# Score units in bursts of three instead of pairs, and four gates made by GpSimd

## The reference

```python
x = L0_attn_query
xn = _layernorm(x, axis=-1)
s = _L0_attn_ref(xn, ..., L0_attn_Wqkv, L0_attn_Wproj, L0_attn_bproj)   # softmax(q k / 4) v, then Wproj
g = _silu(_L0_ffn_ref(xn, ..., L0_ffn_proj1, L0_ffn_proj1_bias, L0_ffn_proj2, L0_ffn_proj2_bias, L0_ffn_gate_w))
x = x + s * g
```

## Time and profile before

| | us |
|---|---|
| median of 3 runs | 140.52 (140.23 to 141.25) |
| profiled execution | 139.67 |
| its span, first to last instruction | 137.9 |
| TensorE busy | 123.3 (89%) |
| VectorE busy | 88.0 (64%) |
| ScalarE busy | 75.9 (55%) |
| GpSimd busy | 50.8 (37%) |

### The profile page before, as it was taken

The page is one execution under the profiler, slowest core; times in us unless marked ns, Lnnn a source line. Parts: engine busy times, 40 slices in busy tenths (PEclk is TensorE's granted clock), DMA queues, the critical chain, the costliest instruction groups (busy, mean ns, idle before and its releaser), DMA issues.

```text
span 137.9 us, 2606 instructions
## 1 busy us (share of the span) xinstructions
PE 123.3 (89%) x980; PEld 93.9 (68%) x980; DVE 88.0 (64%) x178; ACT 75.9 (55%) x115; POOL 50.8 (37%) x53
## 2 busy tenths in 40 slices
PE   6669979999999699999999995899999999999640
PEld 5359868988899498886776783575666657656340
DVE  0658964300004599999996999096567838857563
ACT  3054359879971101137747432969779698779010
POOL 3268205999991000006466620299021000022300
PEclk9999999999999999999999999999999999999975
DMA  4899799999999950000000003500000100100202
GB/s 128 220 422 420 186 161 174 170 187 190 200 198 203 198 99 15 0 5 2 0 0 0 12 5 114 197 0 13 11 0 31 49 0 19 62 2 18 65 2 76
DMA packets 7553, 13.29 MB, mean 96 GB/s; under 512 B 1012, under 2 KB 2676, under 8 KB 7284
## 3 DMA queue, kind: packets, MB, share of 16 engines
q1 hardware_dynamic: 7108, 12.85, 38.9%
q10 hardware_dynamic: 432, 0.27, 1.1%
HBM read 5.51 MB, written 1.05 MB: 48 GB/s over the span
## 4 chain that ended last, share of the span: by engine, by line
PE 66%; DVE 15%; ACT 6%; issue 5%; DMA 5%; SPq 1%; ACTq 0%; DVEq 0%
PE bank L574 45%; PE bank L690 9%; DVE negm L491 8%; PE bank L662 6%; PE bank L642 6%; DMA wqkv_raw<-wqkv 5%; ACT PT L419 3%; DVE cd L508 2%; DVE yh L535 1%; ACT cTh L431 1%; DVE fin L553 1%; ACT xTh L363 1%; DVE rc L511 1%; SPq L247 1%; ACT wqh L353 0%
## 5 line engine op out<-in xcount | busy, mean ns | idle before, releaser
L491 DVE TENSOR_REDUCE negm<-bank 128x4 f32<-128x1024 f32 x32 | 37.1, 1218 | 20.1 <-PE bank L642 20.0
L419 ACT ACTIVATE PT<-bank 128x1024 f32<-128x1024 f32 x32 | 30.9, 1018 | 7.5 <-PE bank L662 7.5
L328 POOL TENSOR_TENSOR hTl<-hG,hTh 128x512 fp32r<-128x512 f32 x16 | 20.3, 1298 | 26.7 <-ACT hTh L405 26.7
L338 POOL TENSOR_TENSOR bg<-gate,bps 128x256 f32<-128x256 f32 x8 | 6.1, 762 | 38.6 <-DVE gate L459 29.9
L690 PE MATMUL bank<-PT,VA 128*17 128x256 f32 x256 | 16.9, 382 | 0.0
L574 PE MATMUL bank<-w2h,hTh 128*128 128x256 f32 x64 | 14.8, 313 | 1.8 <-DVE yh L535 1.6
L425 ACT ACTIVATE th<-yh 128x256 f32<-128x256 f32 x8 | 3.3, 417 | 22.9 <-DVE yh L535 22.9
L508 DVE STREAM_TRANSPOSE cd<-bank 128x256 f32<-128x256 f32 x16 | 7.2, 448 | 13.3 <-PE bank L690 13.3
L662 PE MATMUL bank<-qs,ks 50*128 50x256 f32 x128 | 12.9, 311 | 2.4 <-DVE negm L491 1.9
L574 PEld LDWEIGHTS bank<-w2h,hTh 128*128 128x128 f32 x64 | 9.7, 190 | 7.1 <-issue 6.1
L401 ACT ACTIVATE hG<-bank,b1s 128x512 f32<-128x512 f32 x16 | 11.0, 690 | 5.5 <-PE bank L574 5.5
(11 more groups left out here) (72 smaller groups left out, 205.2 us busy)
## 6 DMA issues: line engine op xcount, KB each, us to landing
qs<-stage SPq DMA_DIRECT2D x12, 256.0 KB, 10.6
ks<-stage SPq DMA_DIRECT2D x12, 256.0 KB, 16.1
w_raw<-w SPq DMA_DIRECT2D x2, 1024.0 KB, 10.3
xs<-x SPq DMA_DIRECT2D x4, 256.0 KB, 5.9
xb<-x SPq DMA_DIRECT2D x1, 1024.0 KB, 5.2
out<-fin SPq DMA_DIRECT2D x8, 128.0 KB, 1.7
wqkv_raw<-wqkv SPq DMA_DIRECT2D x3, 256.0 KB, 6.8
wps<-wp SPq DMA_DIRECT2D x8, 32.0 KB, 8.7
```

The costliest lines, as they stand in the source:

```text
L328: nc.gpsimd.tensor_tensor(hTl[:, n % FC, :], hG[:, n % FC, :], hTh[:, n % FC, :].bitcast(f32), ALU.subtract).then_inc(h_lo, 1)
L338: nc.gpsimd.tensor_tensor(bg[:, u % 2, :], gate[:, u, :], bps[:], ALU.mult).then_inc(bg_done, 1)
L419: nc.scalar.activation(PT[:, w % 4], scores_of(*s), ACT.Exp).then_inc(exp_done, 1)
L491: nc.vector.tensor_reduce(negm[:, j, :, :, s[1] % 2, b].rearrange("p q a -> p a q"), scores_of(*s), axis=AX.X, op=ALU.max, negate=True).th ...
```

## The change

1. `build_order` cuts the 32 score units into bursts of three (ten of three and one of two) and spreads the same filler over the 11 bursts. MT 0 and MT 1 are put ahead of the scores of a burst, two bursts behind the one that has their last maximum.
2. GpSimd makes the gates of tiles 0 to 3, as th + 1 and then times yh, in its own loop over the list, between the low parts of F1. VectorE keeps those of tiles 4 to 7. The semaphore gate_done becomes gate_first and gate_late, and the final product waits for the gate explicitly.

```diff
--- before.py
+++ after.py
@@ -20,6 +20,7 @@
 STM = STK + 2
 WARM = 5
 AHEAD = 6
+BURST = 3
 VW = HN + 1
 PAIRS = [(j, b) for half in range(2) for j in range(HP // 2) for b in (2 * half, 2 * half + 1)]
 
@@ -40,17 +41,17 @@
     filler = [(s, 1) for s in ffn[:4 * TT // 2]] + [(("F1", n), 1.9) for n in range(FC, 2 * FC)]
     filler += [(s, 1) for s in ffn[4 * TT // 2:4 * TT // 2 + AHEAD]]
     ffn = ffn[4 * TT // 2 + AHEAD:]
-    share = sum(w for _, w in filler) / len(PAIRS)
-    at = 0
-    for n in range(len(PAIRS)):
+    bursts = [range(n, min(n + BURST, 2 * len(PAIRS))) for n in range(0, 2 * len(PAIRS), BURST)]
+    share = sum(w for _, w in filler) / len(bursts)
+    at, turn = 0, [[], []]
+    for n, burst in enumerate(bursts):
         while filler and at < (n + 1) * share - 0.5:
             step, w = filler.pop(0)
             order.append(step)
             at += w
 
-        order += [("S", 2 * n), ("S", 2 * n + 1)]
-        if n >= 2 and PAIRS[n - 2][1] == B - 1 and PAIRS[n - 2][0] < 2:
-            order.append(("MT", PAIRS[n - 2][0]))
+        order += [("MT", j) for j in turn.pop(0) if j < 2] + [("S", u) for u in burst]
+        turn.append([PAIRS[u // 2][0] for u in burst if u % 2 and PAIRS[u // 2][1] == B - 1])
     assert not filler
     for g in range(GROUPS):
         j, b = divmod(g, B)
@@ -189,8 +190,9 @@
         m_rows = [sem(f"m_rows{j}") for j in range(HP // 2)]
         pv_made, cd_out, rc_done, norm_done = (sem(n) for n in ("pv_made", "cd_out", "rc_done", "norm_done"))
         turned, ct_hi, ct_lo, wp_hi, wp_lo = (sem(n) for n in ("turned", "ct_hi", "ct_lo", "wp_hi", "wp_lo"))
-        f2_made, b2_half, yh_done, th_done, gate_done, bg_done, xb_done = (
-            sem(n) for n in ("f2_made", "b2_half", "yh_done", "th_done", "gate_done", "bg_done", "xb_done"))
+        f2_made, b2_half, yh_done, th_done, gate_first, gate_late, bg_done, xb_done = (
+            sem(n) for n in ("f2_made", "b2_half", "yh_done", "th_done", "gate_first", "gate_late", "bg_done", "xb_done"))
+        th_plus = sem("th_plus")
         pj_made, gated, fin_done = sem("pj_made"), sem("gated"), sem("fin_done")
 
 
@@ -234,6 +236,10 @@
 
         def scores_of(*s):
             return bank[:, home[s][0]:home[s][0] + 2, :].rearrange("p a (q c) -> p a q c", q=2)
+
+        def gate_of(u):
+
+            return (gate_first, u + 1) if u < TT // 2 else (gate_late, u - TT // 2 + 1)
 
         block = ctx.enter_context(nc.Block())
 
@@ -323,16 +329,24 @@
                 fs = slice(4 * q, 4 * q + 4)
                 nc.gpsimd.tensor_tensor(w2l[:, fs, :], w2_raw[:, fs, :], w2h[:, fs, :].bitcast(f32),
                                         ALU.subtract).then_inc(w2_lo, 1)
-            for n in range(2 * FC):
-                pool.wait_ge(h_hi, n + 1)
-                nc.gpsimd.tensor_tensor(hTl[:, n % FC, :], hG[:, n % FC, :], hTh[:, n % FC, :].bitcast(f32),
-                                        ALU.subtract).then_inc(h_lo, 1)
+            for s in order:
+                if s[0] == "F1":
+                    n = s[1]
+                    pool.wait_ge(h_hi, n + 1)
+                    nc.gpsimd.tensor_tensor(hTl[:, n % FC, :], hG[:, n % FC, :], hTh[:, n % FC, :].bitcast(f32),
+                                            ALU.subtract).then_inc(h_lo, 1)
+                elif s[0] == "F2" and s[2] == 3 and s[1] < TT // 2:
+                    u = s[1]
+                    pool.wait_ge(th_done, u + 1)
+                    nc.gpsimd.tensor_scalar_add(th[:, u % 2, :], th[:, u % 2, :], 1.0).then_inc(th_plus, 1)
+                    pool.wait_ge(th_plus, u + 1)
+                    nc.gpsimd.tensor_tensor(gate[:, u, :], th[:, u % 2, :], yh[:, u % 2, :], ALU.mult).then_inc(gate_first, 1)
             pool.wait_ge(wp_hi, 1)
             nc.gpsimd.tensor_tensor(wpl[:], wps[:], wph[:].bitcast(f32), ALU.subtract).then_inc(wp_lo, 1)
             pool.wait_ge(x_again, 16)
             pool.wait_ge(bias_in, 48)
             for u in range(TT):
-                pool.wait_ge(gate_done, u + 1)
+                pool.wait_ge(*gate_of(u))
                 if u >= 2:
                     pool.wait_ge(xb_done, u - 1)
                 nc.gpsimd.tensor_tensor(bg[:, u % 2, :], gate[:, u, :], bps[:], ALU.mult).then_inc(bg_done, 1)
@@ -421,7 +435,7 @@
                     u = s[1]
                     act.wait_ge(yh_done, u + 1)
                     if u >= 2:
-                        act.wait_ge(gate_done, u - 1)
+                        act.wait_ge(*gate_of(u - 2))
                     nc.scalar.activation(th[:, u % 2, :], yh[:, u % 2, :], ACT.Tanh).then_inc(th_done, 1)
                 elif s[0] == "TURN":
                     kc, j = s[1:]
@@ -457,7 +471,7 @@
                 dve.wait_ge(yh_done, u + 1)
                 dve.wait_ge(th_done, u + 1)
                 nc.vector.scalar_tensor_tensor(gate[:, u, :], th[:, u % 2, :], 1.0, yh[:, u % 2, :],
-                                               ALU.add, ALU.mult).then_inc(gate_done, 1)
+                                               ALU.add, ALU.mult).then_inc(gate_late, 1)
 
             nc.vector.memset(warm[:], 0.0).then_inc(warm_set, 1)
             norm_stats(0)
@@ -531,10 +545,10 @@
                         dve.wait_ge(v_made, 4)
                     dve.wait_ge(f2_made, u + 1)
                     if u >= 2:
-                        dve.wait_ge(gate_done, u - 1)
+                        dve.wait_ge(*gate_of(u - 2))
                     nc.vector.scalar_tensor_tensor(yh[:, u % 2, :], bank_of("F2", u, 0)[:, 0:E], 0.5, b2s[:],
                                                    ALU.mult, ALU.add).then_inc(yh_done, 1)
-                    if u >= 1:
+                    if u > TT // 2:
                         finish_gate(u - 1)
                 elif s[0] == "GATE":
                     finish_gate(TT - 1)
@@ -546,6 +560,7 @@
                 elif s[0] == "PJ" and s[2] == KC - 1:
                     u = s[1]
                     dve.wait_ge(pj_made, u + 1)
+                    dve.wait_ge(*gate_of(u))
                     dve.wait_ge(xb_done, u + 1)
                     if u >= 4:
                         dve.wait_ge(stored[u - 4], 16)
```

## The result

The changed kernel takes 148.55 us (median of 4 runs, 147.99 to 150.99) against 140.88 (4 runs, 140.23 to 143.15): ratio 1.055, 95% interval 1.047 to 1.062, slower by 7.7 us. Ratios and intervals leave out executions more than 1.5% above the fastest of their kernel (eight of the ten with the gates alone, three of the four with place 4 mended); medians and ranges are of all. The forecast was 145.5 with a range up to 148.3: the direction is right, the time lies outside. The profiled execution is the longest of the four (150.99 us, span 149.1 against 137.9), so its delays are somewhat larger than those of the median.

The account below looks back on a forecast made before the run. VectorE and TensorE bound the scores stretch in turns, TensorE the rest. Start +0.72, gates -1.32 and idle +5.9 gave +5.3, the walk +5.15, taken as +5.1: 144.8 profiled, 145.6 with the median's 0.85, stated 145.5; range 142.3 to 148.3.

Parts of the forecast that it names:

- place 4: yh of tile 4 stands behind maximum 29, delaying F2(5,0) and S30: VectorE idle 2.4 us, TensorE about 2.7.
- The units and the walk: Unit times carried through the scores order: first maximum 0.72 us later, last maximum at 91.65 against 86.49, +5.15 us.
- Place 1: yh of tile 0 stands behind three maxima, F2(1,0) waits for its bank: TensorE waits 2.9 us, VectorE idles 3.1.
- place 3: MT0 now follows F1 14 and 15, so VectorE waits for mm's copy on ScalarE: 1.7 us idle.
- the middle: Scores between maxima 3 and 23 come late at several bursts: VectorE idle 1.5 us in sum, perhaps nothing.
- Gates: GpSimd makes the gates of tiles 0 to 3 in 1.5 to 1.6 us a tile, hidden, with nothing added.
- The term of -1.32 us for VectorE: Four gates of 0.33 us leave VectorE's queue in the scores stretch, saving 1.32 us.
- I let it give nothing back: Second stage, behind the last maximum: order unchanged, TensorE 92% busy, length stays 51 us, so the delay carries through.
- The x reload and the DMAs of maxima: Steps issued earlier against ST0: DMAs cost nothing; x, 3 us earlier, may move the ctxn product by a few tenths.
- rival A: TensorE's clock falls at stops near 45.3 and 84.4 us, slowing work ahead of scores: +1.2 to +3.0, 147.5 us; chance 0.22.
- Rival B: Bursts keep VectorE fed in the scores stretch and its idle time goes to nothing: -3.4, 137.1 us; chance 0.06.
- C: The second stage's own chain gives back most of the delay, about no change: 140.5 us; chance 0.05.

Follow-up runs that it names:

- the gates alone: Kernel before, its list of score pairs kept, with only the gates of tiles 0 to 3 moved to GpSimd: 142.74 us, ratio 0.998.
- place 4 mended: Changed kernel with F2(4,3) moved ahead of S27 to S29: 146.71 us, no ratio given.
- bursts only: Kernel before with the new list of bursts of three, all gates staying on VectorE: 150.49 us, ratio 1.072.
- one place mended: Two kernels: the changed kernel with another bank for F2(1,0), 145.36 us, or with F2(4,3) moved ahead of S27 to S29, 146.71 us.
- three filled stops: Changed kernel with unread matmuls added in TensorE's stops ahead of F2(1,0), F2(5,0) and ST0: 144.60 us, ratio 1.027.
- every place mended: Changed kernel with another bank for F2(1,0), F2(4,3) ahead of S27 to S29 and MT0 ahead of S22: 141.58 us, ratio 1.008.
- the pairs: Kernel before with GpSimd's gates and another bank for F2(1,0): 140.15 us, ratio 0.994; with 12 unread matmuls ahead of ST0, 138.77 us.

## Why the prediction was right and where it failed

- **The units and the walk: right.** With the clock held, M is 47.22 to 47.26, and the first maximum starts 0.75 later than in the kernel before (43.99 against 43.24, forecast 0.72), in one execution each; with the list of bursts it starts anywhere from 43.04 to 46.02 in the other traces. M was to be 91.65 - 43.96 = 47.7. The order's own cost is 47.24 - 43.25 + 0.75 = 4.7 us by the traces, and 144.60 - 140.88 = 3.7 us by the medians; forecast 5.1 to 5.15. In M the half microsecond is spread over all the idle places, each 0 to 0.2 shorter than in the walk.
- **Place 1 (yh 0), place 4 (yh 4), place 3 (MT0), the middle: right** in cause and size, each seen by name. Place 1 measured 3.1 us and place 4 1.6 by their edits; place 3 gave back 0.8 of its 1.5.
- **Gates: right for GpSimd.** 0.86 + 0.73 and the gap make 1.67 us a tile (forecast 1.5 to 1.6), and nobody waits. The term of -1.32 us for VectorE was not measured by itself in bursts at full clock: the gates alone shorten M by 0.22 in the list of pairs, and in the list of bursts, with both falls, by 0.34 (51.45 against 51.79).
- **"I let it give nothing back", the second stage unchanged at 51 us: failed** in the changed kernel (53.66), right wherever the clock stayed up (50.8 to 51.5). The x reload and the DMAs of maxima had no part: with the same list and a full clock E is 51.09.
- **The step that failed is the clock, put at nothing in the sum** and left to rival A. I gave A 0.22 and 1.2 to 3.0 us, and took as forecast that it would not happen because the stop at 84.1 to 87.0 had not caused one. It is in the profile of the change twice; of the six traced stops of 2.60 to 2.96 us ahead of F2(1,0) and F2(5,0), in the changed kernel, in bursts only and in those with one place mended, five have a fall in them or within 2 us behind them. And its price was taken from the filler that stands directly behind each stop. The clock stayed down for about 10 us, over the next burst and its filler as well (4.18 and 4.03 us in place of 2.35 each) and through the first 8 us of the second stage, where TensorE is the bound. Measured as the difference to three filled stops it is 148.55 - 144.60 = 3.9 us in the median; in the profiled execution, the longest, 51.45 - 47.22 = 4.2 in the scores stretch and 53.66 - 51.09 = 2.6 behind it. With 3.9 in place of 0 and 4.7 for the order the forecast would have been 145.5 - 0.4 + 3.9 = 149.0, near the 148.55 found; that the sum closes says that no large term is missing, but it is no forecast, since both were measured afterwards. The time found lies inside what I had given A (up to 148.6).
- **Rival B** (faster) and **C** (given back) did not come about. With every place mended M is 41.73, 1.5 us below the kernel before. 1.32 of that is what the gates took out of VectorE's queue, so its idle time is about what it was; the bursts did not make it go to nothing, as B had it.

Not settled: why a stop of 2.95 us let the clock fall in two traces and not in a third; whether the gates on GpSimd make executions with a low clock more frequent (mean clock 0.944 or lower in 6 of 10 with the gates alone, in 5 of 14 of the kernel before beside them); and whether VectorE's shorter queue could bring more with a fuller TensorE. The other three executions of the changed kernel, 2.3 to 3.0 us shorter, were not traced, so how many falls they had is not known.

## What to carry to other kernels

When work is grouped into longer bursts on one engine, look first at what small step stands behind the burst in the in-order queue of the next engine and who needs its result: here two yh and one copy cost 6.8 us of idle time. Changing one bank and two positions took 5.5 us off M. When a walk gives an engine new stops of 2 to 3 us on TensorE, price the half clock behind them as part of the forecast, not as a rival, and over all that TensorE does while it lasts: about 10 us each time in the changed kernel. A gain in one stretch is only kept if the stop at its end doesn't cost the clock of the next: here a dozen unread matmuls took E from 52.34 to 51.42 in the pairs, and the ratio from 0.994 to 0.983, with intervals that overlap a little.

## What the runs showed of the hardware

- 46 additional matmuls made the kernel faster by 3.4 us (148.55 to 145.10); the granted clock in the scores stretch was 1.00 with them and 0.87 without. The Trainium skill ("TensorE: Matmul & The Clock Gate", Part 1) says that activity releases the half clock, and the runs agree.
- The length of the stop alone did not tell whether the clock falls. Stops of 2.96 and 2.95 us at the same place had 0.50 behind them once and 1.00 once. TensorE's stop at ST0 was 1.18 us both with the gates alone (clock 1.00 in the 20 us behind the last maximum) and in the pairs with the other first bank (0.91).
- On GpSimd adding a constant to 128x256 (one tensor in) took 0.86 us, longer than the product of two tensors of that size, 0.73. I had taken both at 0.74.
